# Two of eight row tiles of the last expert combination on GpSimd, and a new order of the output's stores

## The reference

```python
x = x + 0.5 * ffn(layernorm(x))       # 16 experts, top 2, and a shared one
x = x + attention(layernorm(x))       # 16 heads of 16, causal, with a distance penalty
x = x + 0.5 * ffn(layernorm(x))       # the same weights again
```

```python
routed = jnp.einsum('tke,tk,teh->th', oh, w, y)
shared = jax.nn.silu(xt @ sWg) * (xt @ sWu) @ sWd
return routed + shared
```

## Time and profile before

| what | value |
|---|---|
| median of 3 runs | 376.84 us (375.06 to 377.88) |
| profiled execution | 375.6 us |
| its span, first to last instruction | 373.9 us |
| mean granted TensorE clock | 0.877 |
| busy: PE, DVE, ACT, POOL | 271.8, 253.1, 159.3, 122.9 us |
| instructions: DVE, POOL | 833, 148 |
| additions of line 1220 | 32, 16 of them from 364.1 us on |
| stores of line 461 | 8, from 365.7 to 371.7 us |

### The profile page before, as it was taken

How to read it: one execution, slowest core, us unless ns; L and a number is a source line. 1 busy time by engine, 2 the same in 40 slices (tenths; PEclk the granted TensorE clock), 3 DMA queues, 4 the chain that set the end, 5 groups by cost and what they waited for, 6 DMA issues and landing times.

```text
span 373.9 us, 6430 instructions
## 1 busy us (share of the span) xinstructions
PE 271.8 (73%) x1891; PEld 195.1 (52%) x1891; DVE 253.1 (68%) x833; ACT 159.3 (43%) x413; POOL 122.9 (33%) x148
## 2 busy tenths in 40 slices
PE   2647549978882698679999898996373797898810
PEld 1437419868770277234444444664362486787700
DVE  8776966666573995998888885566830366576616
ACT  3667505444351173335566567653220144444400
POOL 6028823555564042750000000000177024554530
PEclk9955959999996699869999999999685599999975
DMA  7999555435204326662332220000022603334028
GB/s 244 382 383 300 187 152 187 124 110 147 91 2 123 102 83 213 163 180 88 84 78 72 65 48 1 2 2 1 11 103 99 183 29 122 103 122 128 31 64 273
DMA packets 30207, 45.63 MB, mean 122 GB/s; under 512 B 5789, under 2 KB 23371, under 8 KB 29790
## 3 DMA queue, kind: packets, MB, share of 16 engines
q1 hardware_dynamic: 25582, 36.24, 31.6%
q0 software_dynamic: 4592, 8.98, 6.9%
HBM read 27.98 MB, written 20.61 MB: 130 GB/s over the span
## 4 chain that ended last, share of the span: by engine, by line
PE 42%; DVE 20%; DMA 11%; SPq 10%; issue 7%; ACT 5%; another core or an unknown queue 3%; POOL 1%; DVEq 0%; POOLq 0%
PE bank L303 27%; SPq L422 5%; DMA stk_q<-parts_d 5%; PE bank L846 4%; DVE bank L1298 4%; DVE wl L1062 3%; PE bank L770 3%; DMA w_raw<-in_experts 3%; DVE res L1220 2%; DMA yg<-results 2%; PE bank L901 2%; PE bank L914 2%; PE bank L755 1%; PE bank L938 1%
## 5 line engine op out<-in xcount | busy, mean ns | idle before, releaser
L532 POOL DMA_INDIRECT results<-ysb,xb x62 | 61.0, 984 | 75.1 <-DVE ysb L1201 56.9
L1298 DVE CUSTOM_DVE_ANT_0 bank<-bank,dec 128x512 f32<-128x512 f32 (+3 forms) x128 | 59.6, 512 | 11.0 <-PE bank L901 10.6
L721 ACT ACTIVATE ct<-bank 128x512 f32<-128x512 f32 (+1 forms) x96 | 45.8, 528 | 37.1 <-PE bank L918 36.5
L1162 DVE TENSOR_TENSOR hm<-sg,bank 128x128 f32<-128x128 f32 x78 | 22.3, 285 | 50.8 <-ACT sg L592 28.6
L592 ACT ACTIVATE sg<-bank 128x128 f32<-128x128 f32 x78 | 21.6, 277 | 66.4 <-PE bank L303 53.7
L521 POOL DMA_INDIRECT slots_x<-xn,slot x32 | 34.3, 1071 | 32.4 <-DVE slot L1139 23.4
L901 PE MATMUL bank<-stk_q,stk_k 96*128 96x512 bf16 (+3 forms) x128 | 37.0, 326 | 9.3 <-DMA stk_q<-parts_d 4.6
L303 PE MATMUL bank<-wh,xT_h 128*128 x124 | 40.3, 325 | 3.3 <-DVE xT_l L1189 2.7
L638 ACT ACTIVATE xT_h<-bank 128x256 fp32r<-128x256 f32 x62 | 23.8, 385 | 34.3 <-PE bank L846 27.8
L770 PE MATMUL bank<-ident,hm 128*128 128x128 f32 x78 | 23.7, 303 | 19.7 <-issue 16.9
L303 PE MATMUL bank<-wh,hT_h 128*128 (+1 forms) x78 | 30.6, 392 | 8.2 <-DVE res L1179 3.1
(11 more groups left out here) (173 smaller groups left out, 679.7 us busy)
## 6 DMA issues: line engine op xcount, KB each, us to landing
xb<-slots_x SPq DMA_DIRECT2D x62, 128.5 KB
w_raw<-in_experts SPq DMA_DIRECT2D x17, 384.0 KB, 7.8
yg<-results SPq DMA_DIRECT2D x16, 256.0 KB, 4.5
slots_x<-zeros SPq DMA_DIRECT2D x2, 1285.0 KB, 12.0
parts_d<-part SPq DMA_DIRECT2D x6, 384.0 KB, 3.2
stk_k<-parts_d SPq DMA_DIRECT2D x8, 192.0 KB, 3.4
stk_q<-parts_d SPq DMA_DIRECT2D x8, 192.0 KB, 3.8
slots_x<-zeros SPq DMA_DIRECT2D x1, 1413.5 KB, 7.8
```

Of the source, the lines that this page charges most:

```text
L532: pool.indirect_dma_start(results, where, ysb[c % RING][:], None, bounds_check=4 * N - 1, oob_is_err=False).then_inc(s_ys[c % RING], 16)
L721: act.activation(ct[n % 6][:, a:b], bank[2 + i][:, 0:b - a], ACT.Exp).then_inc(s_exp, 1)
L1298: dve.tensor_tensor_reduce(s_i, s_i, dec[:, SEQ - w:SEQ], 1.0, NEG, ALU.add, ALU.max, mmax[g % 2][:, n % G * QT + i:n % G * QT + i + 1])\
```

## The change

VectorE keeps row tiles 0, 1, 3, 4, 6 and 7 of the last combination, in pairs (0, 1), (3, 4), (6, 7), with the same instructions. Tiles 2 and 5 go to GpSimd, after its last scatter. GpSimd first multiplies both halves of `yg[t]` in place with their gates (two `tensor_scalar` with a column of `gate`), then adds the first half to `res` and then the second (two `tensor_tensor`), with a link after the multiplications and after the first addition. It raises a new semaphore `s_cmp` when a tile is done. SP's queue stores the tiles in the order 0, 1, 3, 4, 2, 6, 7, 5 and waits for `s_cmp` or `s_cmb` before each. The combination of the first `ffn` is as before.

```diff
--- before.py
+++ after.py
@@ -244,6 +244,7 @@
         s_yg = [sem(f"s_yg{i}") for i in range(NT)]
         s_cm0 = sem("s_cm0")
         s_cmb = sem("s_cmb")
+        s_cmp = sem("s_cmp")
         s_was = [sem(f"s_was{i}") for i in range(3)]
         s_wah = sem("s_wah")
         s_wap = sem("s_wap")
@@ -295,6 +296,7 @@
         v_bank = [4, 6, 5, 7] * 2
         o_bank = [(5, 1), (2, 3)]
         NH = B * H
+        pool_tiles, dve_tiles = (2, 5), (0, 1, 3, 4, 6, 7)
 
         def three(eng, to, xs, ws, ins):
 
@@ -456,8 +458,11 @@
             attention()
             blocks(1)
             load_results(1)
-            for t in range(NT):
-                sp.wait_ge(s_cmb, NT + t + 1)
+            for t in (0, 1, 3, 4, 2, 6, 7, 5):
+                if t in pool_tiles:
+                    sp.wait_ge(s_cmp, pool_tiles.index(t) + 1)
+                else:
+                    sp.wait_ge(s_cmb, NT + dve_tiles.index(t) + 1)
                 sp.dma_start(out_v[:, t, :], res[:, t, :]).then_inc(s_out, 16)
             sp.wait_ge(s_out, 16 * NT)
 
@@ -558,6 +563,13 @@
 
             scatter(1)
             scatter_results(1)
+            for t in pool_tiles:
+                pool.wait_ge(s_yg[t], 32)
+                for k in range(2):
+                    ins = pool.tensor_scalar(yg[t][:, k, :], yg[t][:, k, :], gate[:, k, t:t + 1], None, ALU.mult)
+                link(ins)
+                link(pool.tensor_tensor(res[:, t, :], res[:, t, :], yg[t][:, 0, :], ALU.add))
+                pool.tensor_tensor(res[:, t, :], res[:, t, :], yg[t][:, 1, :], ALU.add).then_inc(s_cmp, 1)
 
         @block.scalar
         def _(act):
@@ -1384,8 +1396,16 @@
             for r in (2, 3):
                 turn_low(3, r)
             ffn(1)
-            for r in range(NP_):
-                combine(1, r)
+            for i in range(0, len(dve_tiles), 2):
+                for k in range(2):
+                    for j, t in ((i, dve_tiles[i]), (i + 1, dve_tiles[i + 1])):
+                        if k == 0:
+                            dve.wait_ge(s_yg[t], 32)
+                        else:
+                            dve.wait_ge(s_cm0, NT + j + 1)
+                        dve.scalar_tensor_tensor(out=res[:, t, :], in0=yg[t][:, k, :], scalar=gate[:, k, t:t + 1],
+                                                 in1=res[:, t, :], op0=ALU.mult, op1=ALU.add)\
+                            .then_inc((s_cm0, s_cmb)[k], 1)
 
 
 # ---- launch: arrays laid out so that a partition's words lie together in DRAM
```

## The result

The changed kernel took 384.76 us (median of 4 runs, 383.43 to 386.72), the kernel before 375.95 us (4 runs, 374.76 to 377.88): ratio 1.0221, 95% interval 1.0172 to 1.0271. So it is slower, clear of the noise, by 1.7 to 2.7%; the medians are 8.8 us apart. I had predicted 378.7, up to 380.9, and called it no change. The profiled execution has a span of 382.9 us against 373.9.

The account below looks back on a forecast made before the run. The tail after the last scatter was taken as limited by VectorE and yg's loads, nearly level. VectorE 1.45 us later plus 0.4 us of store gave +1.85 on 376.84, so 378.7 us; range 375.7 to 380.9.

Parts of the forecast that it names:

- GpSimd does nothing after its last scatter [...], so nothing stands in front: Tail: GpSimd idle from 361.1 at the latest, so the moved tiles' work waits for no earlier GpSimd work.
- my rivals: Tail: no blocking, 377.1 us, chance 0.15; VectorE keeps its turn, 379.1, 0.15; dear GpSimd multiplication, 381.3, 0.12.
- The multiplication on GpSimd: Tiles 2 and 5: each 128x256 multiplication by a gate column takes 0.395 us, priced from GpSimd's one-input casts.
- The high end of 1.16: Tiles 2 and 5: upper price in us of each GpSimd multiplication, that of a two-input 128x512 operation; total 381.3 us.
- my schedule: Tail: instruction-by-instruction timetable of both engines; GpSimd's last addition ends at 371.98, VectorE's last at 373.13.
- The turns: Tail: VectorE and GpSimd block each other and alternate, multiplications included; VectorE ends 1.45 us later; chance 0.52.
- The sum: Tail: VectorE's end 1.45 us later plus 0.4 us for one more store issue, +1.85 us.
- the last VectorE addition ends near 373.1: Tail: sign of being right, VectorE's end in the profile if the engines take turns.
- the loads are only 0.2 us ahead of VectorE: Tail: tile 7 lands at 370.2, VectorE starts it at 370.4; relieving VectorE undisturbed gains only 0.2 us.
- +2.8 us: Tail: the sum if blocked instructions waited out whole durations one after another, in place of +1.85.
- the tail from the last scatter to the end is not between 0 and 4 us longer: Tail: the stated sign that the prediction is wrong, compared with the kernel before.

Follow-up runs that it names:

- early_drain: Kernel before plus a 128x1 GpSimd memset waiting for VectorE's last addition, and an extra DRAIN right behind the last scatter; tail from last scatter to end 13.86 us.

## Why the prediction was wrong

**What failed** is a step of few words: "GpSimd does nothing after its last scatter [...], so nothing stands in front". I costed what stands in front of the moved work and not what stands behind it. Behind it is the DRAIN, which before had 5.7 us to spare against the last landing, and after is moved by 14.9 us with GpSimd's last work. From the traces: 13.61 + 7.85 + 0.24 to the end = 21.7, where the last store alone gives 16.0 (15.91 and 16.16 without the DRAIN). So 5.7 of the 7.8 us in the tail are the DRAIN, 2.1 the rest. None of my rivals had it; the range left it out too. The 2.1 are GpSimd's own late work, as the runs without the DRAIN say: with the multiplications on ScalarE half of the 2.1 goes, and with them on GpSimd the last store goes out 0.02 to 0.03 us behind GpSimd's last addition.

**The multiplication on GpSimd**: 0.395 us taken, 0.92 to 1.01 measured in the changed kernel, 0.96 alone. The error is that casts stood for it. The high end of 1.16 held it. That GpSimd and not SP's order of stores gives the last store follows from it: GpSimd ends at 13.5 to 14.1, where my schedule had 371.98 - 359.96 = 12.0. In the profiled execution it works from 6.28, when tile 2 has landed, to 13.61, with no gap longer than the 0.08 us of its links: 7.3 us where the schedule had 5.7.

**The turns.** That they exist was right, and their price came from the right rows, but not who takes part. VectorE's additions are stretched to 0.95 us, as I had said (0.8 to 1.1), only where a GpSimd addition runs, two of them in the changed kernel's profile:

```profile
369.72 0.95 DVE L1406 SCALAR_TENSOR_TENSOR res<-yg,gate,res 128x256 f32<-128x256 f32 x1
```

```profile
373.32 0.95 DVE L1406 SCALAR_TENSOR_TENSOR res<-yg,gate,res 128x256 f32<-128x256 f32 x1
```

In the tails of all traces 22 of VectorE's additions start while a GpSimd addition runs. Every one ends 0.28 or 0.29 us behind it and takes 0.52 to 0.95 us, whenever it starts; my schedule had 0.35 behind it. Beside GpSimd's tensor_scalar, from 367.52 to 369.46, VectorE's at 368.19 took its 0.48, as the row shown above says. Of 44 that start while a multiplication runs, 32 took 0.47 to 0.50 us and 12 took 0.62 to 0.72; what decides that stays open. The multiplications in turn took 0.92 to 1.37 us there, against 0.96 alone.

The Trainium skill (SBUF — State Buffer, "Who interferes with whom"), which the prediction cites, has a GpSimd instruction that reads SBUF contend with a two-input one of VectorE for ports that are an exclusive lock. The traces agree for the addition. For the multiplication, which reads SBUF too, they do not: 32 of 44 were not held up.

**The sum** without the DRAIN was +1.85 us; the runs give 16.0 against 13.9 and 14.1, +1.9 to +2.1. The size is right by two errors against each other: the multiplication was too cheap by 4 x 0.56 us, and the turns too many, six additions of VectorE held up in the schedule where two were. That the two meet is luck. So is one of my signs of being right, "the last VectorE addition ends near 373.1": it ended at 13.03, 373.0 on that scale, but because tiles 5, 6 and 7 landed 1.0 us later than in the kernel before and its last addition took 0.95. Of GpSimd's four additions two took over 0.8 us, as I had said, and two 0.79. That the change cannot gain, because the loads are only 0.2 us ahead of VectorE, was right: in the changed kernel VectorE waits for a load before each group of additions, 0.98, 0.25, 1.13 and 0.24 us from tile 3 on. With 12 additions VectorE ends from 11.51 to 13.03, with all 16 and no GpSimd work beside them from 11.50 to 12.69.

**Slips in the working.** The two stretches of the earlier trace rows count an addition at their common border twice: VectorE has 16 instructions in the tail and not 17. The "+2.8 us" for whole durations one after another is VectorE's delay alone; with the store's 0.4 it is 3.2. Neither changes the forecast.

**The sign of being wrong** that I had named, "the tail from the last scatter to the end is not between 0 and 4 us longer", is what came: it is 7.8 longer.

## What to carry to other kernels

Before an engine gets work later than it had, look at everything that its queue still holds behind its last busy instruction, the closing DRAIN above all: it counts as idle in the busy tables, and an engine that looks free may have its end hidden with no more than a few us to spare. In a kernel that, like this one, issues many DMAs from GpSimd, late work on GpSimd has this price, unless a DRAIN is put where GpSimd is idle and others are not, as early_drain did for the tiny late operation; for the changed kernel it was not tried at that place. And if the engine to be relieved waits for loads, as VectorE here, taking a quarter of its work away gained nothing that the traces show.

## What the runs showed of the hardware that I had not expected

GpSimd's DRAIN takes about 0.083 us for each indirect DMA that GpSimd issued since its last DRAIN (94, 47 and 31 of them: 7.84, 3.91 and 2.60 us), and 0.05 us when there was none; after 16 it took 2.26 and 2.36, more than that. All of them have 128 row indices, so whether the time goes by DMAs or by indices is not told apart. A 128x256 f32 tensor_scalar of GpSimd takes 0.96 us with a column and 0.85 with a constant, a tensor_tensor of the same size 0.64 to 0.72. Beside VectorE the latter took up to 0.91. A two-input addition of VectorE that starts during such a tensor_tensor of GpSimd ends 0.28 us behind it, which stretches it from 0.48 to as much as 0.95 us. During a tensor_scalar of GpSimd 32 of 44 were not stretched, and 12 to 0.62 to 0.72.
